# Second attention: the order of the small jobs on the shared PSUM bank

## The reference, cut to what matters

```python
mixed_q = hidden_states @ wq + bq                       # jobs XT, Q; K and V likewise
glo = jnp.mean(mixed_q, axis=1, keepdims=True)
c = jnp.tanh(mixed_q @ wfq + bfq + (glo @ wfg + bfg))   # jobs GB, F
p, z = jnp.sum(c * up[None], -1), jnp.sum(c * uz[None], -1)           # job PZ
P, Z = jax.nn.sigmoid(p) * key_len, jax.nn.sigmoid(z) * key_len
G = -(j[None, None, None, :] - P[..., None]) ** 2 * 2.0 / Z[..., None] ** 2   # job CF
probs = jax.nn.softmax(q @ k.T / sqrt(D) + G, axis=-1)
ctx = probs @ v                                         # jobs ctx0 to ctx3
x = layernorm(x + ctx @ wo + bo)                        # jobs CT, OUT, then norm
```

## Time and profile before

| | us |
|---|---|
| median of 3 executions | 1611.47 |
| lowest and highest | 1609.98, 1611.98 |
| the profiled execution | 1612.34 |
| its span, first to last instruction | 1610.6 |
| of it, second attention's passes with scores | 1046.9 to 1520.3 |
| the six passes of the loop | 57.87 to 58.92 each |

### The profile page before, as it was taken

One profiled execution on the slowest core, in us unless ns is written; L12 is line 12 of the kernel. 1 busy time (PEld: TensorE's weight loads), 2 busy tenths in 40 slices (PEclk: granted clock), 3 DMA queues, 4 the chain that ended last, 5 costly groups with the idle time before them and its releaser, 6 DMA issues. The chain is left out here.

```text
span 1610.6 us, 37407 instructions
## 1 busy us (share of the span) xinstructions
PE 1448.2 (90%) x12185; PEld 808.4 (50%) x12185; DVE 1116.6 (69%) x2581; ACT 956.0 (59%) x2056; POOL 755.3 (47%) x944
## 2 busy tenths in 40 slices
PE   5999999999999999999978998878888888887837
PEld 3666666666666666666655666522333332332225
DVE  5567666666757657666677777778888888888732
ACT  2555555555555555555556887737667677675721
POOL 4656656655665665665564444511222231232633
PEclk9999999999999999999989999959999999999968
DMA  6101000000100000000000000150111111111000
GB/s 193 26 21 28 22 20 23 23 20 20 26 20 20 26 20 20 22 25 20 20 17 2 0 0 1 37 156 24 51 33 36 43 33 49 36 36 34 18 24 17
DMA packets 71099, 50.82 MB, mean 32 GB/s; under 512 B 30875, under 2 KB 59408, under 8 KB 70896
## 3 DMA queue, kind: packets, MB, share of 16 engines
q1 hardware_dynamic: 67936, 45.70, 10.3%
q10 hardware_dynamic: 1760, 3.02, 0.6%
q0 software_dynamic: 1344, 1.33, 0.3%
HBM read 38.18 MB, written 13.28 MB: 32 GB/s over the span
## 5 line engine op out<-in xcount | busy, mean ns | idle before, releaser
L608 ACT ACTIVATE prob<-score_ps,nmax 128x512 f32<-128x512 f32 (+3 forms) x512 | 266.8, 528 | 181.7 <-DVE nmax L669 181.7
L669 DVE TENSOR_REDUCE nmax<-score_ps 128x1 f32<-128x512 f32 (+3 forms) x512 | 225.0, 481 | 200.2 <-PE score_ps L488 195.4
L1932 DVE TENSOR_REDUCE a_nm<-a_s 128x1 f16<-128x512 f32 x512 | 324.0, 685 | 46.1 <-PE a_s L1768 43.6
L1890 ACT ACTIVATE a_pt<-a_st 128x1024 f32<-128x1024 f32 x256 | 261.7, 1024 | 122.1 <-PE a_st L1772 121.3
L1768 PE MATMUL a_s<-a_kop,a_qop 64*128 64x512 f16 x512 | 185.0, 405 | 62.6 <-DVE a_nm L1932 54.6
L786 POOL TENSOR_SCALAR_AFFINE_SELECT k_h<-k 64x512 f16<-64x512 f32 x130 | 79.1, 609 | 266.7 <-ACT k L635 256.4
L500 PE MATMUL pt_ps<-ident,prob 128*128 128x128 f32 x1280 | 186.2, 276 | 2.4 <-ACT pt L617 1.4
L617 ACT ACTIVATE pt<-pt_ps 128x512 f32<-128x512 f32 (+1 forms) x192 | 102.9, 536 | 139.4 <-PE pt_ps L500 139.4
L1772 PE MATMUL a_st<-a_qop,a_kop 64*128 64x512 f16 x512 | 175.1, 395 | 0.0
L1804 PE MATMUL a_pv<-a_pt,a_vaug 128*32 128x256 f32 x2048 | 167.4, 399 | 8.0 <-ACT a_pvs L1895 6.1
L789 POOL TENSOR_TENSOR k_l<-k,k_h 64x512 f16<-64x512 f32 x130 | 152.6, 1174 | 10.8
(11 more groups left out here) (376 smaller groups left out, 3038.6 us busy)
## 6 DMA issues: line engine op xcount, KB each, us to landing
r_bc<-r_parts SPq DMA_DIRECT2D x128, 128.0 KB, 2.8
a_qop<-q_parts SPq DMA_DIRECT2D x64, 64.0 KB, 1.9
a_kop<-k_parts SPq DMA_DIRECT2D x64, 64.0 KB, 1.9
x_tok<-in_L_attn_input_dram SPq DMA_DIRECT2D x4, 512.0 KB, 12.4
r_parts<-rsum SPq DMA_DIRECT2D x128, 2.0 KB, 2.1
q_parts<-a_q_h SPq DMA_DIRECT2D x16, 128.0 KB, 2.3
k_parts<-a_k_h SPq DMA_DIRECT2D x16, 128.0 KB, 2.3
e_w<-in_L_ffn_w_dram SPq DMA_DIRECT2D x1, 2048.0 KB, 10.5
```

The lines of the kernel that those rows point to most:

```text
L608: ins = nc.scalar.activation(prob[h][:, P_OFF[c]:P_OFF[c] + w], score_ps[u][:, col:col + w], ACT.Exp, bias=nmax[h][:, c:c + 1], accum_out= ...
L669: ins = nc.vector.tensor_reduce(nmax[h][:, c:c + 1], score_ps[u][:, col:col + P * (c + 1)], AX.X, ALU.max, negate=True)
L1890: nc.scalar.activation(pt[kc % 2][r][:, :, :], st_ps[r][:, :, :], ACT.Exp, scale=1.0 / SC).then_inc(exp_done[r], 1)
L1932: nc.vector.tensor_reduce(nm[g % 2][:, c, hh:hh + 1], s_ps[j][:, :], AX.X, ALU.max, negate=True).then_inc(max_done[j], 1)
```

## The change

Five jobs and `norm` change place in a pass; no instruction is added or taken away.

| | before | after |
|---|---|---|
| ctx3 | 8E | 7E |
| F | 7E | 8E |
| CT | 9M | 9E |
| PZ | 9E | 10M |
| OUT | 10M | 10E |
| ctx0 | 12E | 11E |
| CF | 11E | 12E |
| norm | behind 11E | behind 12M, after nm2 |

```diff
-MIDDLE = {4: "nm0", 8: "nm1", 9: "CT", 10: "OUT", 12: "nm2", 13: "RX", 15: "RD"}
-END = {0: "ctx1", 1: "XT", 2: "Q", 3: "RC", 4: "ctx2", 5: "K", 6: "GB", 7: "F", 8: "ctx3", 9: "PZ", 11: "CF", 12: "ctx0",
-       13: "V", 14: "RL", 15: "nm3"}
+MIDDLE = {4: "nm0", 8: "nm1", 10: "PZ", 12: "nm2", 13: "RX", 15: "RD"}
+END = {0: "ctx1", 1: "XT", 2: "Q", 3: "RC", 4: "ctx2", 5: "K", 6: "GB", 7: "ctx3", 8: "F", 9: "CT", 10: "OUT", 11: "ctx0",
+       12: "CF", 13: "V", 14: "RL", 15: "nm3"}
...
                         if at in table:
                             shared_use(table[at], kind, b)
-                    if at == 11 and behind:
-                        step("norm", b - 1)
+                        if at == 12 and half == 0 and behind:
+                            step("norm", b - 1)
```

## The result

The changed kernel took 1616.32 us in the median of six executions (1615.73 to 1617.48), the kernel before 1611.56 (1607.77 to 1613.07) in the six beside them. The ratio is 1.0034, with a 95% interval of 1.0021 to 1.0047: slower by 0.34%, clear of the measurement. The forecast was 1615.4 and slower. The profiled execution took 1617.48, with a span of 1615.7 against 1610.6.

What follows compares the result with a forecast made beforehand. In the second attention PE and DVE were taken to bound the kernel as a pair locked through single score banks. Loop +4.0, last pass +0.5 and first pass -0.9 gave +3.6 us, forecast 1615.4 us, range 1610.2 to 1618.9.

Steps and rivals of the forecast that it cites:

- the walk: Loop pass from 9M to the start of 14M, priced half-slot by half-slot: 21.39 us after the change, 20.73 before.
- The step's sum: Half-slots 9M to 14M of one loop pass: +0.66 us a pass, +4.0 us over six passes.
- The lost head start: CT at 9E and RX at 13M: each loses 0.46 us, taking XT's 2.96 instead of 2.50.
- ctx3 and F: Half-slots 7E and 8E: their lengths together stay the same, priced at 0, by bounds -0.1 and +0.1.
- First and last pass: First pass: -0.9 us, as F leaves the low-clock stretch, else up to +1; last pass, 7E to 12E and RX: +0.5.
- The clock: PE's clock falls behind OUT in the loop: three kept, 0.81 us each, bounds none (-2.4 us) and six (+2.5).
- The item behind the stage: The tail behind the second attention: same jobs in the same order, priced at 0.
- rival 1: At CT and RX: the earlier context pays, both keep 2.50, -2.0 us in all, or 1609.5; chance 0.20.
- The earlier context: The claim of rival 1: ctx3 four half-slots before CT instead of one, RX no longer following a context.
- neither in all: Loop passes: the clock holds with no fall, the forecast's mechanism otherwise, 1613.0 us; chance 0.10.
- nor in none: Loop: clock falls in each pass, or first pass stays low longer; 1617.9 us, with the latter up to 1619; chance 0.12.
- the seam: Between two passes: CF's later copy delays SP's loads and the next first score; 1 us over costs 7, 1622; chance 0.03.

Runs made afterwards that it cites:

- The exchange alone: The kernel before with ctx3 at 7E and F at 8E, nothing else moved; ran once, 1629.47 us beside 1628.17 for the kernel before.

## Why the prediction was right

**The pass, by half-slots.** In the loop the mechanism held at each point of the walk. 9M came at 1.20 (forecast 1.20), CT at 3.04 (2.96), PZ 2.52 (2.53), OUT and 11M 4.29 (4.30), ctx0 2.22 (2.22), norm over nm2 2.22 (2.23), 12E 1.20 (1.20), RX 3.03 (2.96), V 1.79 (1.79). The step's sum was +0.66 a pass, the measured one +0.79. Of the difference 0.14 is CT's and RX's: I took XT's chain for theirs, and XT's is 1.93 from transposes to next maximum where CT's and RX's are 2.00. That row was there, in CT's own half-slot before. The lost head start is shown as the cause by four runs, not only argued: CT's half-slot follows the distance of its transposes through 0.50, 0.68, 0.69 and 1.04, whatever stood ahead of it, and unread PE work alone moved it from 1.04 to 0.68.

**ctx3 and F** were priced at 0 within 0.1; with CT gone from behind them they cost 0.02, as measured from 7E to 9M. Alone they cost 0.2 a pass through CT's half-slot, which the full change hides.

**First and last pass.** First: 60.01 instead of 60.77, -0.76 for a forecast of -0.9. The size is right, the reason only in part. I gave all of it to F's leaving the low clock, and F's half-slot did go from 3.32 to 1.86; but 7E, now without a job, still took 2.05, and 8M 1.88 instead of 1.24, since the clock rises at the same time as before, 33 us into the pass, and so only in 8M. From 7E to 9E the pass gained 0.29, and from 9E to 13E, at full clock throughout, 0.36. Before, and then after:

```profile
1077.21:1084.50 7.29, 7.11 (x55) 1.87 (x53) 5.12 (x9) 5.13 (x6) 0.00 (x0) 0.80 0.11 33
1084.50:1098.52 14.02, 11.92 (x116) 4.47 (x116) 11.48 (x21) 9.91 (x13) 3.12 (x10) 1.00 0.04 10
```

```profile
1077.68:1084.68 7.00, 6.93 (x55) 1.74 (x53) 5.08 (x8) 5.10 (x6) 0.00 (x0) 0.77 0.13 39
1084.68:1098.34 13.66, 11.92 (x116) 4.47 (x116) 11.38 (x23) 9.85 (x13) 3.12 (x10) 1.00 0.01 2
```

The exchange alone, which moves F and leaves PZ, CF and ctx0, took 6.89 and 14.13 in these stretches: F's move brings the first gain and not the second. That -0.9 came so near is partly luck. Last: +0.61 between 7E and 13E for a forecast of +0.5, but the pass as a whole was only 0.1 longer, since the clock was low at other half-slots of the routing steps ahead of 7E.

**The clock** is the term most mis-sized. I kept three falls, the number before, by bounds of none and six; five came in the profiled execution. The row that shows PE idle behind OUT is the same as before. In the loop's first pass the fall follows it; in the fourth PE was idle for 1.52 and the clock held.

```profile
1148.65 0.39 PE L1768 MATMUL a_s<-a_kop,a_qop 64*128 64x512 f16 x1 [1.54 <-DVE a_nm L1932]
```

The Trainium skill (TensorE: Matmul & The Clock Gate, What's actually happening) says that the window by which the clock is set runs freely and doesn't start with the kernel. The runs agree in so far as the clock held in some passes and fell in others of the same run, behind the same idle time at OUT. How much of the step from three falls to five is the change's own doing is open: each count is from one execution, with XT at 1M it was six, and no second profile of one kernel shows how far the count varies by itself. That it does is likely: in one set the mean clock of the kernel before ranged from 0.962 to 0.968 over its 19 executions, and one fall more or less changes that mean by about 0.001 (other parts of the program change it too).

Over the six passes 357.20 - 6 x 58.82 = 4.3 us came on top of the full-clock length, before 350.20 - 6 x 58.03 = 2.0; 0.2 of the 2.3 between them is PZ's longer half-slot in the loop's first pass, the rest the falls. A fall's price was also too high in my bounds: I read 0.81 from 10M to 12E, but over the whole pass the three falls before cost 0.54, 0.72 and 0.89 (58.57, 58.75 and 58.92 against 58.03). A fall also costs more or less by what runs at the low clock: from 10E to 13E the loop's first pass took 14.13 us against 12.96 at full clock, with ctx0's four f32 transposes in it.

```profile
1144.82:1158.95 14.13, 11.02 (x95) 3.84 (x92) 11.40 (x31) 7.92 (x11) 7.54 (x19) 0.88 0.08 23
...
1323.83:1336.79 12.96, 9.87 (x99) 3.69 (x96) 11.26 (x31) 8.19 (x11) 7.54 (x19) 1.00 0.08 24
```

**The account.** In the spans: +0.6 ahead of the stage, -0.8 first pass, +4.7 placing in six passes (0.79 each), +2.3 clock and PZ's longer half-slot, +0.1 last pass, -1.7 behind it (91.6 to 89.9 us, where no instruction moved), +5.1 in all. The item behind the stage I had at 0 and did not expect. All profiled kernels have the same work there, and those of the faster sets take 89.9 to 91.6 us for it; the two compared here happen to be the ends of that. So the direction and the placing's price are the mechanism's, but that the forecast of +3.6 came near the measured +4.8 is partly luck: the placing was 0.7 too low and the clock 2.3, and the tail's -1.7 took back over half of that. (The range's lower end, 1610.2, lies above rival 1's 1609.5, not at its middle, as I wrote; the result lies at the other end.)

**Rivals.** The earlier context pays nothing: the exchange alone has the context farther off, and CT is dearer. The clock held in one pass of six, neither in all nor in none. No wait arose at the seam: SP's last load is issued at 1340.42 and the next pass starts at 1345.55, so over 4 us of cover are left, as worked out.

```profile
1340.42 0.90 SPq L1374 DMA_DIRECT2D a_kop<-k_parts  x2
```

## What to carry to other kernels

Where two engines feed each other through single buffers, a side job's price depends on which of the two is ahead when it comes: measure from the buffer's reader to the job's start, and put a job with a long chain directly behind one that has put the producer ahead, rather than spreading jobs with quiet stretches between them. Walk a table of placements through the lengths that the trace shows for the same neighbours; that reached the pass within 0.13 us of 59. And keep a single consumer's long run of operations off the point where the matmul engine waits for it, since the idle time may cost its clock as well.

## What was not expected of the hardware

- The clock can fall without one long idle: with PE's longest wait behind OUT cut from 1.54 to 0.81 us, three of six equal passes still fell, alternating, at 0.8 us each; with XT moved as well, none did in the profiled execution.
- Equal passes fall or don't: three of six before, and six of six with XT at 1M, in one profiled execution each. The fall's place moves from pass to pass: 1.08 us into 11M, then 0.54 into 11M, then 0.98 into 10E in the kernel before, each time behind the same idle of 1.54 us.
- 0.59 us of extra PE work in a stage with PE busy 86% of a pass (50.5 of 58.8) was free in one place (12E) and cost 0.13 in another (9M).
